# DLRM tower on one Trainium2 core: own embT slots for tiles 2 and 3, weights loaded and split later

## What is computed

```
e = stack([tbl_f[ids[:, f]] for f in range(27)], axis=1)        # 2048 x 27 x 128
inter = einsum('bfd,bgd->bfg', e, e)                            # per sample 27 x 27
x = inter[:, f, g] for g < f                                    # 351 pairs
h = concat([bottom, x, bottom], axis=1)                         # 607 columns
h = maximum(h @ W_top1 + b_top1, 0)                             # 607 x 512
h = maximum(h @ W_top2 + b_top2, 0)                             # 512 x 256
y = h @ W_top3                                                  # 256 x 1
```

## Time and profile before

| | us |
|---|---|
| timed runs, median of 3 (lowest to highest) | 382.67 (381.82 to 383.13) |
| span of the profiled execution | 633.3 |
| TensorE busy in it | 402.0 |
| GpSimd, VectorE, ScalarE busy | 262.1, 254.0, 144.4 |
| mean granted TensorE clock, share of full | 0.827 |

### The profile page before, as it was taken

The page is one execution under the profiler, slowest core; times in us unless marked ns, Lnnn a source line. Parts: engine busy times, 40 slices in busy tenths (PEclk is TensorE's granted clock), DMA queues, the critical chain, the costliest instruction groups (busy, mean ns, idle before and its releaser), DMA issues.

```text
span 633.3 us, 10256 instructions
## 1 busy us (share of the span) xinstructions
PE 402.0 (63%) x4321; PEld 374.0 (59%) x4321; DVE 254.0 (40%) x341; ACT 144.4 (23%) x268; POOL 262.1 (41%) x283
## 2 busy tenths in 40 slices
PE   2207655492738928298465956469392892839997
PEld 2206543492727918197464955469381992829986
DVE  3117955191315704074040921338040560407422
ACT  3204722020302213112311123012130221311521
POOL 6761447317370364505463073712646045550010
PEclk9999967597668969599595996769776896959999
DMA  8812652114221232114121241211321132211021
GB/s 200 174 50 77 175 167 77 52 28 135 55 55 40 64 104 65 41 40 128 35 75 28 45 134 47 61 39 36 127 64 53 36 81 84 64 40 39 9 61 9
DMA packets 44889, 45.76 MB, mean 72 GB/s; under 512 B 32720, under 2 KB 35558, under 8 KB 43948
## 3 DMA queue, kind: packets, MB, share of 16 engines
q1 hardware_dynamic: 33646, 26.52, 16.3%
q0 software_dynamic: 8896, 17.89, 10.9%
q10 hardware_dynamic: 2302, 0.70, 0.5%
HBM read 39.52 MB, written 5.55 MB: 71 GB/s over the span
## 4 chain that ended last, share of the span: by engine, by line
PE 50%; issue 20%; another core or an unknown queue 18%; ACT 5%; DVE 4%; DMA 2%; SPq 0%; ACTq 0%; DVEq 0%
PE work L389 21%; PE gram L416 16%; PE work L401 3%; PE work L442 2%; PE work L443 2%; PE work L444 2%; DVE onehot L536 2%; ACT embT L506 2%; ACT embT L675 2%; DMA inter<-in_tbl 1%; PE work L470 1%; DVE tab_lo L521 1%; DMA misc<-in_bottom 1%; PE work L459 1%
## 5 line engine op out<-in xcount | busy, mean ns | idle before, releaser
L359 POOL DMA_INDIRECT emb<-in_tbl,ids_all x272 | 258.2, 949 | 304.9 <-PE work L401 217.7
L536 DVE TENSOR_TENSOR onehot<-ids_bc,row_idf 125x1024 fp32r<-125x1024 int32 (+2 forms) x232 | 199.4, 921 | 94.0 <-PE work L389 60.9
L416 PE MATMUL gram<-embT 128*54 128x52 f32 x2048 | 110.3, 264 | 161.7 <-issue 134.6
L389 PE MATMUL work<-onehot,tab_hi 125*128 125x256 f32 x672 | 172.8, 296 | 51.2 <-DVE onehot L536 26.0
L416 PEld LDWEIGHTS gram<-embT 128*54 128x54 f32 x2048 | 93.9, 179 | 181.5 <-issue 164.2
L389 PE MATMUL work<-onehot,tab_lo 125*128 125x256 f32 x672 | 169.2, 291 | 0.0
L389 PEld LDWEIGHTS work<-onehot,tab_hi 125*128 125x128 f32 x672 | 133.8, 199 | 57.0 <-DVE onehot L536 32.4
L389 PEld LDWEIGHTS work<-onehot,tab_lo 125*128 125x128 f32 x672 | 134.3, 200 | 0.0
L675 ACT COPY embT<-work 128x512 f32<-128x512 f32 (+1 forms) x41 | 30.4, 795 | 163.5 <-PE work L389 98.9
L569 DVE SCALAR_TENSOR_TENSOR x_lo<-work,x_hi 128x512 fp32r<-128x512 f32 x16 | 11.0, 691 | 103.9 <-ACT x_hi L708 72.6
L683 ACT COPY inter<-gram 118x416 f32<-118x416 f32 x64 | 32.3, 506 | 66.5 <-remote 33.6
(11 more groups left out here) (56 smaller groups left out, 220.9 us busy)
## 6 DMA issues: line engine op xcount, KB each, us to landing
ids_bc<-in_sel_ids SPq DMA_DIRECT2D x7, 1280.0 KB
grams<-inter SPq DMA_DIRECT2D x64, 84.5 KB
emb<-in_tbl,ids_all POOLq DMA_INDIRECT x272
misc<-in_tbl SPq DMA_DIRECT2D x3, 448.0 KB
inter<-in_tbl SPq DMA_DIRECT2D x3, 448.0 KB
ids_bc<-in_sel_ids SPq DMA_DIRECT2D x4, 256.0 KB, 5.2
misc<-in_bottom SPq DMA_DIRECT2D x8, 128.0 KB
raw_hi<-in_tbl SPq DMA_DIRECT2D x1, 560.0 KB
```

What stands on the lines that cost most here:

```text
L359: pool.indirect_dma_start(out=emb[:, t % TILE_SLOTS, f, :], out_offset=None, in_=gather_tables[f], in_offset=bass.IndirectOffsetOnAxis(ap= ...
L389: mm = nc.tensor.matmul(out, part[0:k, CHUNK_AT[f] + c, :], onehot[0:k, at % RING, i * HALF:(i + 1) * HALF], start=(c == 0 and i % 2 == 0 ...
L416: last = nc.tensor.matmul(gram[side * SIDE:side * SIDE + TWO * NF, n % 2, q, 0:COLS], two.rearrange("d s f -> d (s f)"), two[:, :, 0:NG], ...
L536: nc.vector.tensor_tensor(onehot[0:k, at % RING, 0:width], ids_bc[0:k, four[0]:four[-1] + 1, :].rearrange("p i n -> p (i n)"), row_idf[0:k ...
```

## The change

- Tiles 2 and 3 get two slots of their own, `embT_first`, at the address where the split weights, part of `x_hi`/`x_lo` and `h2` lie. The weights are loaded only when grams 2 and 3 are done, into the buffers in which they stay (`raw_w1`, `raw_w2`), and the low part takes the place of the raw values. ScalarE rounds them in half 2, VectorE subtracts.
- The first three halves are written out by hand in the order of each engine. TensorE does grams 0 and 1 and then all three selects of half 1, rows and grams of tile 2, one select of half 2, rows and grams of tile 3, the other two selects, rows and the first half of gram 4, layer one of half 0. The layers of halves 0 and 1 come in halves 2 and later; from half 3 on the order is the old one. The banks are handed out accordingly.
- `ids_bc` is loaded in three parts, each with a semaphore. SP loads those of half 2 behind `store(1)`, and from half 3 on those of the next half behind `store(2h)`, where before all went ahead of it.
- The packed pairs of half 0 are loaded behind the ids of half 2, so behind the last one-hot of half 1.
- The row of ones for the bias moves from 96 to 95, which needs one memset in the place of two; the bias sits in that row.

The diff, without the table of banks, which follows TensorE's order:

```diff
+              nc.sbuf_tensor("embT_first", [P, 2, P, NF], F32) as embT_first):
+            pass
+        with (nc.sbuf_tensor("raw_x", [P, 2, M1 + 2, HALF], F32), nc.sbuf_tensor("raw_w1", [P, 2, CH + 1, H1], F32) as raw_w1,
+              nc.sbuf_tensor("raw_w2", [P, 2, M1, H2], F32) as raw_w2):
...
+        def tile_embT(t):
+            return (embT_first if t in (2, 3) else embT)[:, t % 2, :, :]
+
+        def half_embT(h):
+            return embT_first if h == 1 else embT
...
-            for c in range(2):
-                sp.dma_start(w1_raw[c], w_top1[D + c * P:D + (c + 1) * P, :]).then_inc(w1_loaded[c], 16)
-            sp.dma_start(w2_raw.rearrange("p (c n) -> p c n", n=H2), w_top2.rearrange("(c p) n -> p c n", p=P)).then_inc(w2_loaded, 16)
-            sp.wait_ge(table_hi, NSEL)
-            sp.wait_ge(table_lo, len(PIECES))
-            sp.dma_start(bot[:, :, :], bottom_v[0]).then_inc(bot_loaded, 16)
-            sp.wait_ge(w1_padded, 1)
-            sp.dma_start(w1_raw[2][0:PAIR_ROWS[2], :], w_top1[D + 2 * P:D + PAIRS, :]).then_inc(w1_loaded[2], 16)
-            sp.dma_start(w1_raw[2][ONES:ONES + 1, :], b_top1.rearrange("(o n) -> o n", o=1)).then_inc(w1_loaded[2], 16)
+            def load_ids(h, j):
+                four = FOURS[j][0]
+                some = slice(four[0], four[-1] + 1)
+                sp.dma_start(ids_bc[:, some, :], sel_ids[h][:, some, :].to_broadcast([P, len(four), HALF])).then_inc(ids_bc_loaded[j], 16)
+
+            def load_weights():
+
+                for c in X_ORDER:
+                    if c == CH:
+                        sp.dma_start(raw_w1[:, 1, CH, :], w_top1[0:D, :]).then_inc(w1_loaded[CH], 16)
+                        sp.dma_start(raw_w1[:, 0, CH, :], w_top1[D + PAIRS:, :]).then_inc(w1_loaded[CH], 16)
+                    else:
+                        sp.dma_start(raw_w1[0:PAIR_ROWS[c], 1, c, :], w_top1[D + c * P:D + c * P + PAIR_ROWS[c], :]).then_inc(w1_loaded[c], 16)
+                    if c == CH - 1:
+                        sp.dma_start(raw_w1[ONES:ONES + 1, 1, c, :], b_top1.rearrange("(o n) -> o n", o=1)).then_inc(w1_loaded[c], 16)
+                sp.dma_start(raw_w2[:, 1, :, :], w_top2.rearrange("(c p) n -> p c n", p=P)).then_inc(w2_loaded, 16)
...
+            for j, (four, _, _) in enumerate(FOURS):
+                sp.wait_ge(onehot_ready, max(n for n, (two, _) in enumerate(ONEHOTS[0]) if SETS[0][two][0][0] in four) + 1)
+                load_ids(1, j)
+            sp.wait_ge(table_hi, NSEL)
+            sp.wait_ge(table_lo, len(PIECES))
+            sp.dma_start(bot[:, :, :], bottom_v[0]).then_inc(bot_loaded, 16)
             for h in range(HALVES):
-                if h + 1 < HALVES:
-                    sp.wait_ge(onehot_ready, OH_AT[h + 1])
-                    sp.dma_start(ids_bc[:, :, :], sel_ids[h + 1].to_broadcast([P, NSEL, HALF])).then_inc(ids_bc_loaded, 16)
                 store(2 * h)
+                if 1 < h < HALVES - 1:
+                    for j in range(len(FOURS)):
+                        sp.wait_ge(onehot_ready, OH_AT[h] + max(n for n, one in enumerate(ONEHOTS[h]) if one[0] == j) + 1)
+                        load_ids(h + 1, j)
                 if 2 * h + 2 == TILES - ID_SLOTS:
 
                     is_filled(sp, "rows", 2 * h + 1, NGR - 1)
                     sp.dma_start(ids_all[:, 0:2 * h + 2, :], ids_v[:, ID_SLOTS:, :]).then_inc(ids_loaded[2], 16)
-                if h + 1 < HALVES:
+                if h != 1 and h + 1 < HALVES:
                     is_filled(sp, "bottom", h)
                     sp.dma_start(bot[:, :, :], bottom_v[h + 1]).then_inc(bot_loaded, 16)
                 store(2 * h + 1)
+                if h == 0:
+                    for j in range(len(FOURS)):
+                        sp.wait_ge(onehot_ready, OH_AT[1] + max(n for n, one in enumerate(ONEHOTS[1]) if one[0] == j) + 1)
+                        load_ids(2, j)
+                    sp.wait_ge(ones_ready, 1)
+                elif h == 1:
+                    load_weights()
+                    is_filled(sp, "bottom", 1)
+                    sp.dma_start(bot[:, :, :], bottom_v[2]).then_inc(bot_loaded, 16)
...
             pe.wait_ge(ident_ready, 1)
-            for h in range(HALVES):
-                for j in range(len(SETS[h])):
+            for j in range(len(TWOS)):
+                select(0, j)
+                rows(0, rows_behind(0, j))
+            bottom_rows(0)
+            products(0, range(GRAMS))
+            rows(1, range(NGR))
+            products(1, range(GRAMS))
+            select(1, 0)
+            select(1, 1)
+            select(1, 2)
+            rows(2, range(NGR))
+            products(2, range(GRAMS))
+            select(2, 0)
+            rows(3, range(NGR))
+            products(3, range(GRAMS))
+            bottom_rows(1)
+            select(2, 1)
+            select(2, 2)
+            rows(4, range(NGR))
+            products(4, range(GRAMS // 2))
+            mlp1(0)
+            products(4, range(GRAMS // 2, GRAMS))
+            mlp2(0)
+            mlp1(1, X_ORDER[:1])
+            mlp3(0)
+            mlp1(1, X_ORDER[1:])
+            rows(5, range(NGR))
+            bottom_rows(2)
+            products(5, range(GRAMS))
+            for h in range(3, HALVES):
+                for j in range(len(FOURS)):
                     select(h, j)
                     rows(2 * h, rows_behind(h, j))
-                    if j == bottom_behind(h):
-                        bottom_rows(h)
-                if h > 1:
-                    mlp2(h - 2)
+                bottom_rows(h)
+                mlp2(h - 2)
                 products(2 * h, range(GRAMS))
-                if h > 1:
-                    mlp3(h - 2)
+                mlp3(h - 2)
                 rows(2 * h + 1, range(NGR))
-                if 0 < h < HALVES - 1:
+                if h < HALVES - 1:
                     mlp1(h - 1)
                 products(2 * h + 1, range(GRAMS))
...
-            def split_w1_bottom():
-                dve.wait_ge(w1_bot_loaded, 32)
-                nc.vector.tensor_tensor(w1_bot[0], w1_bot[0], w1_bot[1], ALU.add).then_inc(w1_bot_summed, 1)
-                dve.wait_ge(w1_bot_summed, 1)
-                dve.memset(w1_bot[1][ONES - QS:ONES + 1, :], 0.0).then_inc(w1_padded, 1)
-                dve.memset(packed[ONES - QS:ONES, CH - 1, :], 0.0).then_inc(ones_zeroed, 1)
-                dve.memset(packed[ONES:ONES + 1, CH - 1, :], 1.0).then_inc(ones_ready, 1)
-                nc.vector.tensor_copy(w1_hi[:, CH, :], w1_bot[0]).then_inc(w1_hi_ready, 1)
-                dve.wait_ge(w1_hi_ready, 1)
-                nc.vector.tensor_tensor(w1_lo[:, CH, :], w1_bot[0], w1_hi[:, CH, :].bitcast(F32), ALU.subtract).then_inc(w1_split, 1)
-
             def split_w1(c):
                 k = X_ROWS[c]
-                dve.wait_ge(w1_loaded[c], 32 if c == 2 else 16)
-                nc.vector.tensor_copy(w1_hi[0:k, c, :], w1_raw[c][0:k, :]).then_inc(w1_hi_ready, 1)
-                dve.wait_ge(w1_hi_ready, c + 2)
-                nc.vector.tensor_tensor(w1_lo[0:k, c, :], w1_raw[c][0:k, :], w1_hi[0:k, c, :].bitcast(F32), ALU.subtract).then_inc(w1_split, 1)
+                if c == CH:
+                    dve.wait_ge(w1_loaded[c], 32)
+                    nc.vector.tensor_tensor(raw_w1[:, 1, c, :], raw_w1[:, 1, c, :], raw_w1[:, 0, c, :], ALU.add).then_inc(w1_bot_summed, 1)
+                dve.wait_ge(w1_hi_ready, X_ORDER.index(c) + 1)
+                nc.vector.tensor_tensor(w1_lo[0:k, c, :], raw_w1[0:k, 1, c, :], w1_hi[0:k, c, :].bitcast(F32), ALU.subtract).then_inc(w1_split, 1)
...
+            for n, (j, c) in enumerate(ONEHOTS[0]):
+                one_hot(0, n)
+                if c % PIECE == PIECE - 1 or c == SETS[0][j][2] - 1:
+                    for i in SETS[0][j][0]:
+                        split_piece(PIECE_AT[TABLE_ORDER.index(i), c // PIECE * PIECE])
+            for n in range(len(ONEHOTS[1])):
+                if n == RING:
+                    split_bottom(0)
+                    dve.wait_ge(table_hi, NSEL)
+                    dve.memset(packed[ONES // QS * QS:ONES + 1, CH - 1, :], 1.0).then_inc(ones_ready, 1)
+                one_hot(1, n)
+            for n, (j, c) in enumerate(ONEHOTS[2]):
+                if (j, c) == (1, 0):
+                    split_packed(0)
+                    for g in range(1, NGR, 2):
+                        rows_out(dve, nc.vector.tensor_copy, 3, g)
+                one_hot(2, n)
+            split_bottom(1)
+            for c in X_ORDER:
+                split_w1(c)
+            split_w2()
+            split_h1(0)
+            split_packed(1)
+            split_h1(1)
+            for g in range(1, NGR, 2):
+                rows_out(dve, nc.vector.tensor_copy, 5, g)
+            split_bottom(2)
+            for h in range(3, HALVES):
+                for n in range(len(ONEHOTS[h])):
+                    if h > 3 and n == RING:
...
-            def load_weights():
-                act.wait_ge(table_lo, len(PIECES))
```

(45 more changed lines are left out.)

201 lines of the change are left out of this document (109 added, 92 removed).

## The result

| | before | after |
|---|---|---|
| timed runs, median (lowest to highest) | 382.25 us (381.57 to 383.13, 4 runs) | 398.62 us (397.86 to 399.11, 4 runs) |
| span of the profiled execution | 633.3 | 397.3 |
| time of the profiled execution | not given | 399.09 |

The ratio is 1.0427, 95% interval 1.0404 to 1.045: slower by 16.4 us, where 6.8 were forecast and 392.5 us was the end of the range. A second measurement gave 1.0456 (1.0427 to 1.0485).

The account below looks back on a forecast made before the run. TensorE sets the end, at 381.5 us by its model, with the gathers' chain close at 376. Terms -1.9 + 0.7 - 0.8 + 0.3 + 2.1 + 4.8 + 1.6 = +6.8, so 382.67 becomes 389.5 us; 8-in-10 range 381.3 to 392.5.

Parts of the forecast that it names:

- 0, up to +1: From half 3 on: old order, ids some 4 us later but landing before TensorE's selects want the sixth one-hot.
- Gram 0, -1.9: Start: VectorE splits the bottom earlier, bottom's load behind two id loads costs nothing; -1.9 us, bounds -5.6 to 0.
- Gram 1, +0.7: Start: ScalarE makes all five copies of tile 1, so gram 1 follows gram 0 later; +0.7 us, bounds 0 to 1.5.
- One-hots of half 1, -0.8: Half 1: five one-hots are ready when select 0 starts; -0.8 us, bounds -2 to 0.
- Gram 2, +0.3: Before gram 2: TensorE waits 1.6 us for ScalarE's copies, against 1.3; +0.3 us, bounds 0 to 1.
- Gram 3, +2.1: Before gram 3: no layer one hides the copies, and ScalarE first rounds half 0's packs; +2.1 us, bounds 0.5 to 5.
- Gram 4, +4.8: Before gram 4: ScalarE rounds weights ahead of tile 4's copies, TensorE waits; main term, +4.8 us, bounds 1.5 to 8.
- New half 2, +1.6: Half 2: layer two's split, gram 5's wait of 1.1 and late one-hots of half 3; +1.6 us, bounds 0 to 4.
- rival (1): Gap of 4.8 us also halves TensorE's clock for half a gram and some layer one; 2 us more, 391.5; chance 0.18.
- (2): Gathers set the pace, tile 4's waiting for tile 2's transposes; +2.8 us, 385.5; chance 0.11.
- (3): Start bound by transfers, so 1.77 MB of weights leaving it saves 8.8 us; 380.7; chance 0.17.
- (4): No net change: ScalarE's weight casts come early enough or the start gains more; 382 to 384; chance 0.11.

Follow-up runs that it names:

- the kernel before with late ids: Kernel before, with ids in three loads and, for halves 3 to 7, issued behind the store of tile 2h: 393.59 us, ratio 1.0333.
- the stand-in: Kernel before, with the ids of a half in three loads instead of one, at the old early place: 381.69 us, ratio 0.9995.
- the ids ahead: Changed kernel, with the next half's ids loaded ahead of the store of tile 2h again, in three parts: 387.92 us, ratio 1.0163.
- after again: Changed kernel, unchanged, measured once more beside the kernel before: 398.98 us, ratio 1.0456.
- the packs earlier: Changed kernel with ids loaded ahead of the store, and half 0's packed pairs loaded ahead of half 2's ids: 388.37 us, ratio 1.0175.

## Why the prediction was wrong

**The failed step** is the sentence that from half 3 on the order is the old one except for the ids, which come "some 4 us later" and land in time: "0, up to +1". They come 11.7 us later: the first such load is issued at 147.19 in the kernel before with late ids, at 135.49 in the stand-in, up to which point the two run alike within 0.4 us. For in the old place they went out as soon as the last one-hot of the half was made, and behind `store(2h)` they wait for the rest of the half's selects, layer two and a whole gram. The 4 us had no row behind them, and I never looked up when VectorE was free for the ids. The step also asked whether the sixth one-hot would be ready in time, where each of the sixteen had to be: with 1.15 us against 0.97 VectorE catches up nothing. It cost 8 to 9 us in the profiles and 11.1 in the timed runs, where "0, up to +1" stood. No rival had it. The prediction itself gave both rates (a one-hot 1.13 us, 16 chunks in 15.56 us).

**The other steps** sum to +6.8, and with the ids ahead the kernel was measured at +6.1. That the two are so near is partly luck: the seven parts as measured come to about +4.2, and 2.3 us of half clock, which the forecast put at nothing, fill most of the difference. One by one, with after or, where it is disturbed, the kernel with the ids ahead, against the stand-in:

- Gram 0, -1.9: it starts at 59.88, against 61.98, -2.1 (-1.5 to -3.7 in the profiles of after again, with the ids ahead, and with the packs earlier). The number held, but "I cost that at nothing" did not quite: the bottom's load was the last by 0.56 us, TensorE's wait for it 3.30 us.
- Gram 1, +0.7: it comes 3.07 behind gram 0, against 2.81, +0.3.
- One-hots of half 1, -0.8: the selects of sets 0 and 1 lose nothing, where the stand-in's take 16.89 instead of 15.63, -1.2.
- Gram 2, +0.3: 1.40 of waiting, against 1.60, -0.2.
- Gram 3, +2.1: 1.05, and 0.3 in its transposes, +1.4; in the profiled run of after a wait for the packs and the half clock brought 3 more.
- Gram 4, +4.8: 4.45.
- New half 2, +1.6: gram 5 waits 1.24 for the bottom's low part, where 1.1 was said, and the selects of half 3 take 0.3 more: +1.6.
- The clock, priced at nothing in the forecast and at 2 in rival (1): 2.3 us at gram 4 and layer one with the ids ahead, 1.6 there and 1.6 at gram 3 in after. I had it as one of two ways; it comes on top of the gap each time. "The engine is full right before the gap" was no protection.

**The rivals.** (1) happened and was too small. (2) did not: GpSimd's last gather ends at 352.1 and the last transposes begin at 366.2, 14 us later. (3) did not: the weights' 1.77 MB left the start, and gram 0 came 2.1 us earlier, not 8.8. (4) did not.

**What bounds the kernel.** That TensorE sets the end held, and so did the model: 41.2 us a half against 41.03 (155.53 to 319.66 holds four in the stand-in); gram 1 ended at 75.1 against 74.36, half 7 36.5 against 36.46, the tail 24.5 against 24.6. The claim that the holes "belong to the profiled execution" fell, and no cost of tracing shows: the profiled run of after took 399.09, the others 397.86 to 399.11.

## What to carry to other kernels

When a load is moved behind another step of a queue, look up when its consumer is free for it, and if that consumer is slower per item than the engine it feeds, count the lead it starts with as time: once lost it doesn't come back within the stage. Work on an engine which copies out PSUM belongs behind the copies that TensorE waits for. A gap of 4.5 us there cost its own length and, by the profiles, 1.6 to 2.5 us more in clock.
